# Swapping the order of a weight load and a block of cast-copies on the GpSimd DMA queue of a transformer layer

## The reference

```python
q = (x @ Wq + bq).reshape(b, s, 16, 64)      # the same for k (Wk) and v (Wv)
q = _apply_rope(q, sin, cos); k = _apply_rope(k, sin, cos)
scores = einsum('bqhd,bkhd->bhqk', q, k) * scale + causal_mask
x = _layernorm(x + softmax(scores) @ v @ Wo + bo)
logits = relu(x @ Wr1 + br1) @ Wr2 + br2
tg, ti = top_k(softmax(logits), 2); tg = softmax(tg / 2)
out = silu(x @ Ws1 + bs1) @ Ws2 + bs2
for e in range(8):
    out += sum(tg * (ti == e))[:, None] * (silu(x @ We1[e] + be1[e]) @ We2[e] + be2[e])
return _layernorm(x + out)
```

## Time and profile before

| What | us |
|---|---|
| median of 7 runs | 6320.3 |
| lowest and highest of these runs | 6310.05 and 7122.71 |
| the profiled execution, device time | 6314.53 |
| its span, from first to last instruction of the slowest core (core 4) | 6312.8 |
| spans of the eight cores | 6260.4 to 6312.8 |
| TensorE busy with matmuls, core 4 | 4949.5 |
| ScalarE busy | 1380.1 |
| VectorE busy | 910.1 |
| GpSimd busy | 827.2 |

### The profile page before, as it was taken

How to read it: one execution, slowest core, us unless ns; L and a number is a source line. 1 busy time by engine, 2 the same in 40 slices (tenths; PEclk the granted TensorE clock), 3 DMA queues, 4 the chain that set the end, 5 groups by cost and what they waited for, 6 DMA issues and landing times. The chain is left out here.

```text
span 6312.8 us, 59946 instructions; the slowest of 8 cores (6260.4 to 6312.8 us)
## 1 busy us (share of the span) xinstructions
PE 4949.5 (78%) x22422; PEld 2141.6 (34%) x22422; DVE 910.1 (14%) x1133; ACT 1380.1 (22%) x1746; POOL 827.2 (13%) x702
## 2 busy tenths in 40 slices
PE   0060255554576699999999999999999999999996
PEld 0030011111112344444444444444444444444443
DVE  0020122212133210110110011011001001001104
ACT  0010133333354312112212211211220220121122
POOL 0000111111010000021121121022012112112211
PEclk9985577766677799999999999999999999999997
DMA  9938988888401110100101001010010010100101
GB/s 114 110 94 101 105 97 100 99 98 103 60 2 52 39 47 27 52 29 34 47 27 54 27 34 47 27 49 33 34 47 27 35 46 34 47 27 34 47 34 60
DMA packets 38393, 344.71 MB, mean 55 GB/s; under 512 B 5528, under 2 KB 5977, under 8 KB 14306
## 3 DMA queue, kind: packets, MB, share of 16 engines
q0 software_dynamic: 8208, 159.92, 21.9%
q1 hardware_dynamic: 29906, 180.98, 7.6%
HBM read 492.40 MB, written 159.38 MB: 103 GB/s over the span
## 5 line engine op out<-in xcount | busy, mean ns | idle before, releaser
L897 PE MATMUL pE<-x2bf,w1s 128*128 128x512 bf16 x9216 | 2012.5, 382 | 5.9 <-DMA w1s<-w1bf 5.9
L926 PE MATMUL pE<-h1bf,w2s 128*128 128x512 bf16 x9216 | 1992.0, 379 | 20.0 <-ACT h1bf L908 20.0
L908 ACT ACTIVATE h1bf<-pE,b_sb 128x512 bf16<-128x512 f32 x1152 | 791.8, 687 | 3157.0 <-PE pE L897 3157.0
L897 PEld LDWEIGHTS pE<-x2bf,w1s 128*128 128x128 bf16 x9216 | 906.0, 98 | 1109.7 <-issue 36.3
L926 PEld LDWEIGHTS pE<-h1bf,w2s 128*128 128x128 bf16 x9216 | 900.5, 98 | 1111.5 <-issue 28.3
L958 POOL TENSOR_TENSOR x<-x,tmp 128x512 f32<-128x512 f32 x512 | 648.4, 1266 | 3474.9 <-DVE tmp L949 3474.9
L384 PE MATMUL pS<-xbf,wk 128*128 128x512 bf16 x256 | 72.3, 453 | 574.3 <-DMA wk<-wkr 574.3
L522 ACT ACTIVATE et<-pS,cst 128x1024 bf16<-128x1024 f32 x320 | 385.4, 1204 | 325.9 <-PE pS L507 157.2
L949 DVE SCALAR_TENSOR_TENSOR tmp<-pE,b_sb,wb 128x512 f32<-128x512 f32 x256 | 192.3, 751 | 1586.4 <-PE pE L926 1583.4
L949 DVE SCALAR_TENSOR_TENSOR tmp<-pE,wb 128x512 f32<-128x512 f32 x256 | 177.1, 692 | 1621.1 <-PE pE L926 1621.1
L275 PE MATMUL pX<-identf_s,xstage 128*128 128x128 f32 x128 | 29.9, 414 | 366.7 <-DMA xstage<-x 363.2
(11 more groups left out here) (131 smaller groups left out, 1506.5 us busy)
## 6 DMA issues: line engine op xcount, KB each, us to landing
w1bf<-w1r POOLq DMA_DIRECT2D x18, 4096.0 KB, 119.3
w2bf<-w2r POOLq DMA_DIRECT2D x18, 4096.0 KB, 145.5
w1s<-w1bf SPq DMA_DIRECT2D x72, 1024.0 KB, 5.2
w2s<-w2bf SPq DMA_DIRECT2D x72, 1024.0 KB, 6.5
xstage<-x SPq DMA_DIRECT2D x16, 512.0 KB, 3.7
xres<-x SPq DMA_DIRECT2D x16, 512.0 KB, 3.6
y<-ybuf SPq DMA_DIRECT2D x16, 512.0 KB, 2.6
wv_sb<-wv POOLq DMA_DIRECT2D x1, 2048.0 KB, 18.6
```

Source lines behind the costliest of these rows:

```text
L897: e.matmul(o, l, r, start=st, stop=sp),
L908: e.activation(out=o, in_=i, func=AF.Silu, bias=b), inc=tA)
L926: e.matmul(o, l, r, start=st, stop=sp),
```

## The change

The block that issues the copies of expert j+2 moves from the q part of `emit_projrope` to the k part, behind the load of wk(j). Nothing else changes: the same DMAs, the same sizes, the same engine.

```diff
             if part == "q":
                 wqs, wqi, qtok = wq_ring.load("gpsimd", d["wqr"][j].rearrange("p k c -> p (k c)"))
-                if j + 2 < NE:
-                    precast_expert(j + 2)
                 wq_ring.wait_loaded("tensor", qtok)
                 specs = (("q", wqs, (wq_ring, wqi), q_sb[par], qr_sb[par], bq_sb),)
             else:
                 wks, wki, ktok = wk_ring.load("gpsimd", d["wkr"][j].rearrange("p k c -> p (k c)"))
+                if j + 2 < NE:
+                    precast_expert(j + 2)
                 wk_ring.wait_loaded("tensor", ktok)
```

## The result

The changed kernel is faster. The ratio of its time to that of the kernel before is 0.9912, with a 95% interval of 0.9892 to 0.9932; from the 6314.5 us of the profiled execution before that is 6259 us (6246 to 6272), some 56 us less. The profiled execution after took 6257.77 us, its slowest core (core 3) a span of 6256.1. More than half of these executions of either kernel had cores of one die at a lower granted clock, so the plain medians (6450.73 us of 14 runs after, 6474.75 of 36 before) lie far above these numbers, and the ratios in this document are of the other executions alone.

A forecast was written before the change was run, and what follows sets the result against it. Attention was taken as bound by a chain on the DMA queue: copy, small load, projection and rotation, next issue. Start +25.1, end −80.7 and cold start +2.5 sum to −53.1 us, from 6314.5 to 6261, range 6228 to 6296.

The forecast's parts named there:

- The wait moves: In attention, TensorE's 574.3 us of waits for wk go; waits for wq(1) to wq(7) come instead, about 510 us in all.
- The start: At attention's start, the first moved copy is issued behind wk(0) instead of wq(0), with the queue empty: +25.1 us.
- The gap: Between copies, from a load's landing to the next issue: unchanged near 19.7 us, 0 us, bounds −19 and +11.
- The copies: The seven expert copies in attention keep their mean of 153.4 us: 0 us, bounds −43 and +26.
- The end: At attention's end, 80.7 us of work moves under the last copy; q(7) starts at 1678.2 instead of 1733.76.
- The cold start: The q(7) projection, now after a wait, takes as long as k(6), 9.56 us instead of 7.08: +2.5, bounds 0 and 5.
- Sum: Whole kernel: 25.1 − 80.7 + 2.5 = −53.1 us, giving 6261 us.
- its base: Whole kernel: the sum is set against the profiled execution's 6314.5 us, 5.8 below the median of the runs.
- held by the copies issued behind it: Slower rival in attention: wk(j) shares the engines with following copies and lands only with them; 6339.6 us, chance 0.05.
- the copies did not lengthen by what that rival needs: No-change rival in attention: each copy takes 7.6 us longer, 161 instead of 153.4, about 6308 us; chance 0.06.
- get past them: Far-faster rival in attention: wq(j+1) gets past the copies and the 574.3 us wait goes; 5753 us, chance 0.02.
- The rule of the Trainium skill: On the copies in attention: issuing each later leaves only the start's +25.1, 6340 us; no chance beyond the slower rival's 0.05.

The follow-up runs named there:

- the profiles of the table: Five profiles, means over eight cores: kernel before (first, second repeat) and changed kernel (first, two repeats), both unchanged; the seven-copy chain lasts 1164 us before, 1168 after.
- The first experiment: Against the kernel before, all copies moved behind wk(j) except the first (expert 2, pair 0), left behind wq(0); ratio 0.9925, profiled execution 6243.8 us.
- the repeats: Kernel before and changed kernel each profiled twice more, unchanged; mean chain 1167.3 and 1161.9 us before, 1162.3 and 1164.0 after.
- the second experiment: Against the kernel before, all copies moved behind wk(j) except the last (expert 8, pair 6), left behind wq(6); ratio 1.0033.
- the kernel with the loads ahead: Against the changed kernel, wq and wk loaded one pair ahead, ahead of the copy, with all seven copies still in attention; 5976.16 us in one profiled execution.
- the second repeat of before: Third profile of the kernel before, unchanged; mean chain of seven copies 1161.9 us, first load of w1s 2126.6; the same repeat of after gave 1164.0 and 2071.8.

## Why the prediction came out as it did

The mechanism and its terms held:

- **The wait moves.** Forecast: 12.5 us for wk(0), near 123 for wq(1), 58 to 70 for the rest, about 510 in all. Measured: 12.91, 125.04, 60.45 to 68.49, and 518.7 − 6.08 = 512.6.
- **The start.** Forecast +25.1; measured 486.32 − 462.25 = 24.1. In the profiles of the table the landing that ends the chain comes at 1625 us before and 1651 after, 26 later. The first experiment adds that leaving the first copy early does not win it back: the second copy starts within 5 us of the same time.
- **The gap.** Forecast unchanged at about 19.7. Measured 664.13 − 644.86 = 19.3 at the first and 1530.17 − 1509.95 = 20.2 at the sixth (wk(6) was issued at 1530.17).
- **The copies.** Forecast unchanged. Measured 644.86 − 486.91 = 158.0 and 1679.56 − 1530.76 = 148.8 at the two ends, and the repeats settle the mean.
- **The end.** Forecast: q(7) at 1678.2 with a wait of some 58 us left. Measured 1679.56, after 60.45. That the two times agree within 1.4 us is luck: the chain differs by more than that between cores, as the last section shows. That this term carries the gain is what the second experiment shows: with the last copy put back, q(7) again follows k(6) by 81.2 us and the gain is gone.
- **The cold start.** Forecast +2.5; q(7) took 8.85 us instead of 7.08, +1.8.
- **Sum.** Forecast −53.1 and 6261 us; the profiled executions differ by 56.8, the mean start of the experts by 51.6, the ratio by 56 (43 to 68).

The step that failed is the last one of the sum, its base. "Against the profiled execution's own 6314.5 that is **6261**" adds the change to the time of one execution, and beyond the 5.8 us to the median of seven runs, which it names and drops, neither the sum nor the range of 6228 to 6296 has a term for how far that base moves from execution to execution. It was put at nothing without a reason, although the table ahead of the prediction has a run of 7122.71. The runs showed it as the largest term of all: the median of the unchanged kernel was 6320.3 in 7 runs and 6474.75 in 36, 154 us more, and that of the changed kernel 6450.73, 155 us above the range. These two medians differ by 24 us only, less than half of the change that was forecast. The mechanism has no part in this; the ratio, which leaves the base out, gives 6259. That this is within 2 us of 6261 is luck in part, since its interval is 26 us wide.

A smaller thing is off ahead of the prediction: the end of attention stands there near 1870 us. In the profile before, wo is issued at 1922.6, so attention ended near 1920. No step rested on it.

The rivals: wk(j) was not held by the copies issued behind it (5.9 us at most), the copies did not lengthen by what that rival needs, and wq(j+1) did not get past them. The rule of the Trainium skill that spoke against the move ("DMA: Bandwidth & Descriptors", Rules for kernel authors, issue early and wait late) would have given 6340 us when applied to the copies, and the runs gave 6259. Applied to the small loads instead, in the kernel with the loads ahead, it is borne out: that execution took 338 us less than the profiled one of before (6314.5 − 5976.2).

## What to carry to other kernels

Here a small load shared a DMA queue with a bulk transfer and landed behind it. Swapping the two moved the wait to the next load and left the period alone; what it won and cost was at the two ends, the time the queue stands empty first and the work that must follow the last transfer. So find the chain and price its ends, rather than the row of the wait. And look at how far the runs of the unchanged kernel lie apart before a forecast of 50 us is given as a time. The larger gains lay in taking the load out of the chain (issue it a period ahead) and in cutting the bulk transfer to pieces that fit under the cover of the loads beside it.

## What the runs showed of the hardware that was not expected

- The same bytes copied beside the same work cost 46 us a copy when issued as four DMAs of 4096 KB, and nothing measurable when issued as 1024 KB pieces 27.6 us apart (4220.2 us for seven copies, against 3901.9 for two and 3900.5 for four in pieces, from the first to the last w1s load, with 3899.9 where no copy flows there). Size and spacing were changed together; which of the two does it was not tried.
- GpSimd did not pass the end of the block while its copies were in flight: its last operation ended at 1328.5, TensorE's last matmul of attention at 1468.6, and the next block began at 1584.4, some 4 us after the DMA share had fallen to 0.00. So the expert block is not the only place that waits for the copies, as the description of the kernel before has it. What in the block's end waits was not tried.
- The chain of seven copies differs between cores of one execution by 23 to 61 us (1147.9 to 1170.7 in the second repeat of before, 1130.7 to 1192.1 in that of after), so an agreement to a few us between single cores proves little.
